# A Mamba mixer with a top-2 expert layer: the row statistics of the first layer norm move from VectorE to ScalarE

## What is computed

```python
def _layernorm(x, axis=-1, eps=1e-05):
    m = jnp.mean(x, axis=axis, keepdims=True)
    v = jnp.var(x, axis=axis, keepdims=True)
    return (x - m) / jnp.sqrt(v + eps)

# the mixer, on _layernorm(x)
xz = einsum('bld,ed->ble', h, in_proj_w); x, z = split(xz, 2)     # 2 x 1024 channels
xc = silu(sum_k conv1d_w[:, k] * xp[:, k:k + l, :])               # causal, 4 taps
dt_r, Bc, Cc = split(einsum('bld,ed->ble', xc, x_proj_w))         # 128, 16, 16
delta = softplus(dt_r @ dt_proj_w.T + dt_proj_bias); A = -exp(A_log)
h_t = h_{t-1} * exp(delta_t * A) + (delta_t * x_t) * B_t; y_t = <h_t, C_t>   # scan over the 512 tokens
out = ((y + xc * D_param) * silu(z)) @ out_proj_w.T

x = x + mixer(_layernorm(x))
x = x + experts(_layernorm(x))    # 8 experts, the top 2 of each token, silu(x w1) * (x w3), w2
```

## Time and profile before

| | |
|---|---|
| median of the runs shown | 4304.62 us |
| profiled execution | 4304.38 us, span 4302.6 us |
| busy, whole span | PE 91%, DVE 84%, POOL 60%, ACT 47% |
| mixer | up to about 2420 us |
| experts | from about 2420 us to the end |

### The profile page before, as it was taken

The page is one execution under the profiler, slowest core; times in us unless marked ns, Lnnn a source line. Parts: engine busy times, 40 slices in busy tenths (PEclk is TensorE's granted clock), DMA queues, the critical chain, the costliest instruction groups (busy, mean ns, idle before and its releaser), DMA issues. The chain is left out here.

```text
span 4302.6 us, 72404 instructions
## 1 busy us (share of the span) xinstructions
PE 3894.7 (91%) x25436; PEld 3380.4 (79%) x25436; DVE 3594.8 (84%) x5245; ACT 2043.5 (47%) x4314; POOL 2569.3 (60%) x2169
## 2 busy tenths in 40 slices
PE   6687889889988988898888599999999999999898
PEld 5565677677767776777676499999999999999886
DVE  5999998999999999999999588878878888788500
ACT  7677777777877778777766111111111111111100
POOL 3677778777876787687777244544545545445300
PEclk9888899999999999999998699999999999999999
DMA  4112353554445354535443555555555665655495
GB/s 162 64 40 93 119 174 114 172 165 151 142 157 174 116 167 162 174 111 177 162 150 101 176 187 176 192 182 181 185 176 181 195 184 177 190 176 190 136 331 192
DMA packets 422581, 694.11 MB, mean 161 GB/s; under 512 B 19680, under 2 KB 209760, under 8 KB 414048
## 3 DMA queue, kind: packets, MB, share of 16 engines
q1 hardware_dynamic: 406160, 655.24, 45.8%
q0 software_dynamic: 14768, 34.41, 4.2%
q10 hardware_dynamic: 1440, 1.81, 0.1%
HBM read 668.25 MB, written 45.95 MB: 166 GB/s over the span
## 5 line engine op out<-in xcount | busy, mean ns | idle before, releaser
L635 POOL TENSOR_TENSOR hs<-hs,bc 128x1024 f32<-128x1024 f32 x512 | 1214.5, 2372 | 307.6 <-DVE hs L1347 285.5
L1347 DVE TENSOR_TENSOR_SCAN hs<-dA,pU 128x1024 f32<-128x1024 f32 x512 | 1168.5, 2282 | 44.5 <-ACT dA L754 22.2
L754 ACT ACTIVATE dA<-delta,aneg 128x255 f32<-128x255 f32 x2048 | 852.1, 517 | 36.9 <-DVE hs L1347 33.7
L1146 PE MATMUL pY<-ident,hs 128*128 128x128 f32 x4096 | 566.1, 286 | 237.3 <-POOL hs L635 237.2
L1146 PEld LDWEIGHTS pY<-ident,hs 128*128 128x128 f32 x4096 | 488.4, 147 | 344.7 <-POOL hs L635 167.4
L1330 DVE TENSOR_TENSOR pU<-pZ,bc 128x1024 f32<-128x1024 f32 x512 | 629.7, 1230 | 30.5 <-issue 0.5
L1821 POOL TENSOR_TENSOR hsum<-hT 128x128 f32<-128x128 f32 x168 | 152.9, 910 | 585.1 <-DVE hT L2169 585.1
L1030 PE MATMUL pM<-xnT,win 128*128 128x256 f32 x1680 | 409.7, 400 | 30.9 <-DMA win<-in_w_in 25.1
L1030 PEld LDWEIGHTS pM<-xnT,win 128*128 128x128 f32 x1680 | 331.7, 203 | 80.8 <-issue 28.3
L2033 PE MATMUL ps<-xT,w1s 128*128 128x128 f32 x2688 | 357.8, 276 | 7.3 <-POOL xt L1837 5.3
L2033 PE MATMUL ps<-xt,su 128*128 128x128 f32 x2688 | 357.2, 276 | 0.0
(11 more groups left out here) (347 smaller groups left out, 7374.5 us busy)
## 6 DMA issues: line engine op xcount, KB each, us to landing
ew<-in_w SPq DMA_DIRECT2D x273, 512.0 KB, 4.1
w1s<-in_w SPq DMA_DIRECT2D x96, 1024.0 KB
w3s<-in_w SPq DMA_DIRECT2D x96, 1024.0 KB
w2s<-in_w SPq DMA_DIRECT2D x96, 1024.0 KB
win<-in_w_in SPq DMA_DIRECT2D x128, 512.0 KB, 4.7
bc<-bc_d SPq DMA_DIRECT2D x64, 1024.0 KB, 9.1
w1s<-in_w SPq DMA_DIRECT2D x32, 512.0 KB
w3s<-in_w SPq DMA_DIRECT2D x32, 512.0 KB
```

Source lines behind the costliest of these rows:

```text
L635: pool.tensor_tensor(hs[b][:, :, :], hs[b][:, :, :], bc[:, N + g * PN:N + (g + 1) * PN, :], ALU.mult)\
L754: e = act.activation(dA[k % NB][:, i, 1:T], delta[:, c, 1:T], ACT.Exp, scale=aneg[:, c, n:n + 1])
L1146: m = pe.matmul(pY[c % 2][:, t * P:(t + 1) * P], hs[k % NB][:, i, t * P:(t + 1) * P], ident[:, :], start=g == 0 and i == 0 and t == 0, sto ...
L1347: dve.tensor_tensor_scan(hs[b][:, :, :].rearrange("p n t -> p (n t)"), dA[b][:, :, :].rearrange("p n t -> p (n t)"), pU[:, :, :].rearrange ...
```

## The change

For the statistics that the steps make (those of the tokens of steps 2 to 15; the lead-in makes those of steps 0 and 1 as before) VectorE's `bn_stats` and `bn_aggr` go. In slot 14, behind `copy_z(2)`, ScalarE does for both tiles an Identity with scale -1/512 and an accumulated sum (minus the mean), waits for its own results, a Square with that as bias and an accumulated sum, waits again, and takes the root with 1/512 as scale. The elementwise results go to a buffer that is free by then (`waste`, `xnT`). The root of slot 13 and its table load go. VectorE waits for `sd1` at (15, 1) and not at (15, 0), the Newton step moves back by one place, its last part behind the last slot; the mean's sign turns in `scales`. The second layer norm is unchanged.

```diff
-        LN1S, BACKS, SPS, LNS = 8, 36, 4, 5
+        LN1S_FIRST, LN1S, BACKS, SPS, LNS = 8, 6, 36, 4, 5
...
+            def mean_of(rows, t, mv, to, step):
+                return act.activation(to, rows[:, t, 0:D], ACT.Identity, scale=-1.0 / D, accum_out=mv[:, t, 0:1]).then_inc(step, 1)
+            def squares_of(rows, t, mv, to, step):
+                return act.activation(to, rows[:, t, 0:D], ACT.Square, bias=mv[:, t, 0:1], accum_out=mv[:, t, 1:2]).then_inc(step, 1)
+            def root(mv, sdev, ready):
+                act.activation(sdev[:, :], mv[:, :, 1], ACT.Sqrt, bias=series[:, 2:3], scale=1.0 / D).then_inc(ready, 1)
...
-                    if u == 13 and ln1:
-                        ge(act, var1, s + 3)
-                        act.activation(tiny1[1][:, :], mv1[:, :, 1], ACT.Sqrt, bias=series[:, 2:3]).then_inc(sd1, 1)
                     if 12 <= u <= 15 and front:
                         copy_z(u - 12, f, szf)
+                    if u == SLOTS - 2 and ln1:
+                        ge(act, logits_mm, r + 1)
+                        ge(act, xf_in, 16 * s + 48)
+                        for t in range(TT):
+                            mean_of(xf, t, mv1, waste[t], moment1)
+                        ge(act, moment1, 2 * TT * s + TT)
+                        for t in range(TT):
+                            squares_of(xf, t, mv1, waste[t], moment1)
+                        ge(act, moment1, 2 * TT * s + 2 * TT)
+                        root(mv1, tiny1[1], sd1)
...
+            def variance(ch, mv, tiny):
+                ch.done(dve.tensor_scalar(tiny[0][:, :], mv[:, :, 1], 1.0 / D, EPS, ALU.mult, ALU.add))
...
+            def ln1_next(n, i):
+                if i == 0:
+                    ln1_chain[0] = Chain(ln1_step, 2 * LN1S_FIRST + LN1S * (n - 2))
+                    dve.wait_ge(sd1, n + 1)
+                ch = ln1_chain[0]
+                if i < 4:
+                    newton(ch, tiny1, i)
+                if i == 0:
+                    variance(ch, mv1, tiny1)
+                if i == 4:
+                    scales(ch, mv1, tiny1, 0, scale1, 1.0)
...
-                        if at in ((12, 2), (12, 3), (13, 1), (13, 2)):
-                            ln1(s + 2, ((12, 2), (12, 3), (13, 1), (13, 2)).index(at))
-                        if u == 15:
-                            ln1(s + 2, 4 + g)
+                        if u == 15 and g >= 1:
+                            ln1_next(s + 2, g - 1)
...
                 if ln1_too:
-                    ln1(s + 2, 8)
+                    ln1_next(s + 2, 3)
                 if picks:
-                    for i in range(4):
+                    pick(0)
+                if ln1_too:
+                    ln1_next(s + 2, 4)
+                if picks:
+                    for i in range(1, 4):
                         pick(i)
```

More of the change, by code:

```diff
@@ L233, in mixer @@
         sd1 = sem("sd1")
+        moment1 = sem("moment1")
         xn1 = sem("xn1")
@@ L696, in step @@
                 xcf, szs, szf = xc[1 - odd], sz[odd], sz[1 - odd]
+                waste = [xnT[odd][:, 2 * t:2 * t + 2, :].rearrange("p d q -> p (d q)") for t in range(TT)]
                 def read_dt(i):
@@ L1260, in aggregate, with scales @@
                 ch.done(i)
-            def scales(ch, mv, tiny, n, ready):
+            def scales(ch, mv, tiny, n, ready, sign=-1.0):
                 ch.settle()
                 ch.done(dve.tensor_copy(rs[n][:, :], tiny[4][:, :]))
-                dve.scalar_tensor_tensor(nb[n][:, :], tiny[4][:, :], -1.0, mv[:, :, 0], ALU.mult, ALU.mult)\
+                dve.scalar_tensor_tensor(nb[n][:, :], tiny[4][:, :], sign, mv[:, :, 0], ALU.mult, ALU.mult)\
                    .then_inc(ready, 1)
+            def variance(ch, mv, tiny):
+                ch.done(dve.tensor_scalar(tiny[0][:, :], mv[:, :, 1], 1.0 / D, EPS, ALU.mult, ALU.add))
             ln1_chain = [None]
             LN1_PARTS = 9
+            def ln1_next(n, i):
[9 more added lines that the diff above has]
+                    scales(ch, mv1, tiny1, 0, scale1, 1.0)
+                    assert ch.n == LN1S
             def ln1(n, i):
                 if i == 0:
-                    ln1_chain[0] = Chain(ln1_step, LN1S * n)
+                    ln1_chain[0] = Chain(ln1_step, LN1S_FIRST * n)
                 ch = ln1_chain[0]
@@ L1289, in ln1 @@
                 if i == 8:
-                    scales(ch, mv1, tiny1, 0, scale1)
-                    assert ch.n == LN1S
+                    scales(ch, mv1, tiny1, 0, scale1, -1.0)
+                    assert ch.n == LN1S_FIRST
             def step(s, odd):
```

## The result

The changed kernel took 4334.52 us (median of 4 runs, 4333.73 to 4335.66), the kernel before 4305.80 in the same comparison. The ratio is 1.0068, with a 95% interval of 1.0053 to 1.0082, so the change costs 0.7%. The profiled execution has a span of 4333.3 us, 30.7 more than before.

What follows compares the result with a forecast made beforehand. VectorE's sequence was taken to bound the mixer, with TensorE's backlog fixing when ScalarE is free in tile steps. Terms +35.2, -2.0 and -3.8 gave +29.4 us on a span of 4302.6: 4334 us predicted, range 4310 to 4350.

Steps and rivals of the forecast that it cites:

- T: Moment when ScalarE is free after the third copy of z; claimed fixed by TensorE's backlog in steps 3 to 13.
- the rooms: Time from ScalarE being free to VectorE's multiply of piece 31: 16.5 us over 11 steps, 1.5 us a step.
- row of waits: Second Square's wait for the last scan, 36.9 us in 11 steps; less about 1.85 us each gives 16.5 us.
- C: Time from ScalarE being free to the multiply of piece 31 with the added block: 4.7 us, between 4.1 and 5.4.
- The wait: VectorE at (15, 1) waits for ScalarE's root in steps 3 to 13; 11 x 4.7 - 16.5 = +35.2 us.
- The 3.8 us at the first scans: Waits of the next step's first scan for decays, in five steps, go when VectorE comes later: -3.8 us.
- Steps 0 to 2: Steps without an expert's tile: step 0 gains about 1.1 us, step 1 1.5, step 2 loses 0.6; together -2.0 us.
- The table switch that costs twice: Rival: ScalarE runs empty another 1.28 us at the table load behind an accumulation; 4348 us, chance 0.04.
- The read-outs of 0.6 us: Rival: each accumulated sum on ScalarE costs a small operation and a refill, 0.6 us; 4353 us, chance 0.07.
- The loss taken back inside the step: Rival: a later VectorE waits less for decays and logits, up to 24.6 us go; 4309 us, chance 0.09.
- The rival "faster": ScalarE's freed 2.9 us of slot 13 brings the root in time; VectorE gains up to TensorE's ranks: 4289 us, chance 0.08.

Runs made afterwards that it cites:

- queue edit: One weight load moved ahead in SyncE's queue: on the change 4296.22 us, on the kernel before 4292.61, on the change with ScalarE's block ahead of the `ysum` copy 4271.23.
- both kernels without the wait: The changed kernel with ScalarE's block moved ahead of the `ysum` copy, 4301.78 us; the changed kernel with VectorE's wait and Newton step behind the last slot, 4300.84.

## Why the prediction was right

4334 us were forecast and 4334.52 measured, and most steps hold one by one. That the two agree to half a microsecond is luck: beside the experiments the kernel before ran in 4297 to 4313 us, by the spans the change costs 30.7 us and not 29.4, by the medians 28.7, and a T that came 3.2 us late, which the forecast had not, was made up for in part by other misses (below).

*The bound and T.* In steps 3 to 13 T moved against the step's start by less than 0.3 us in seven, and by 3.2 us in sum over all eleven. VectorE's earlier arrival and ScalarE's freed time don't move it (root of slot 13 off: ratio 1.0001), TensorE's pause does (queue edit on the change: 38 us). The sum of the rooms by the row of waits was 16.5 us; the same eleven measured one by one give 16.4.

*The block.* C was forecast as 4.7 us between 4.1 and 5.4 and is 4.66: 2.90 for the four operations with their read-outs (forecast 3.0 with the two waits), 1.59 for load and root (1.58), 0.17 up to the multiply (0.15). The unknown term was the read-out of an accumulated sum: it has a row of its own, 0.19 to 0.20 us, overlapped by half with the next operation where one follows. The bound from the shortest ScalarE row was the right neighbour. The load starts 0.01 us after the last read-out ends, so there is no drain. The copy of `ysum` ahead of the block waits 2.4 us longer than before on average over these steps, and not 3: a part of ScalarE's freed time goes into the wait for TensorE at the second copy of z (0.96 us in step 6, 10.5 us in eleven steps).

*The wait.* Forecast: 4 to 6 us for the root in each of the eleven steps; measured: 4.0. Forecast for these steps: 35.2 - 3.8 = +31.4; measured: +33.3. The 3.8 us at the first scans came back as said (no such wait is left after the change). The rest is T, late by 3.2 us in sum: 1.6 in step 3 and 2.3 in step 13, where the third z product took 5.4 us and before 3.7, and 1.2 the other way in step 8, where it was the slow one before; it changes from run to run which steps these are. Against that stands 1.0 us in the stretch from the multiply to the next first scan, which is shorter by up to 0.3 us in ten of the eleven steps; why is open. Together: 11 x 4.66 less the room of 16.4 is 34.8, with 3.2 - 3.8 - 1.0 that makes 33.2, the 33.3 but for rounding.

*Steps 0 to 2.* Forecast -2.0, measured -2.6, with the parts wrong. Steps 0 and 1 gained 0.5 and 0.7 and not 1.1 and 1.5 (step 0 also started 0.2 sooner). VectorE came to the multiply of piece 31 only 0.7 us sooner in both; in step 1 a new wait of 0.44 us for decays is a part of that, the rest is open. And in these steps, without `pick` behind them, the later Newton part stands bare (0.2 us more between the last scan and `softplus`). Step 2 gained 1.3 where I had a loss of 0.6, because T came 3.1 us sooner against its step and not 1.28: both table loads and the root count there, since nothing on TensorE holds ScalarE. The rows:

```profile
465.28 0.58 ACT L781 ACTIVATE sz<-pM 128x512 f32<-128x512 f32 x1
465.76 0.63 ACT L688 ACTIVATE xnT<-xf 128x512 f32<-128x512 f32 x1
```

```profile
470.41 1.22 DVE L1370 TENSOR_TENSOR pU<-pZ,bc 128x1024 f32<-128x1024 f32 x1
```

against 470.19 and 473.04.

*The rivals.* The table switch that costs twice falls with the load of 1.28 us alone. The read-outs of 0.6 us fall with their rows. The loss taken back inside the step falls with the doubled Squares: 16 to 21 us for 18.6 us of work. The rival "faster" was priced wrongly, and this is the step of the prediction that failed without harm to the sum: a root in time would have given about 4301 and not 4289, as both kernels without the wait show. I had taken the room above the ranks as gain and had left out that the next step's start is TensorE's too. The advance of 3.2 us from which no step would lose was an average as well: the room between T and the multiply was 0.49 us in steps 8 and 11 and 2.88 in step 3.

## What to carry to other kernels

When work moves to an engine that is idle, look at what its idle time waits for, and put the work ahead of that wait and not behind it: the same block cost 0.7% behind a copy that waits for TensorE and nothing measurable ahead of it. The room that a new wait has is the distance between two rows of the trace, one on each engine, and a row of some later wait often holds it for all steps at once. Before counting a saving on the busiest engine, ask which other engine stands just behind it; here the saving was worth 2.5 us alone, not told from nothing, and 21 us once a 2 us pause of TensorE was gone.

## What the runs showed of the hardware

- A ScalarE operation with an accumulated sum is followed by a row of its own, ACTIVATION_READ_ACCUMULATOR, of 0.19 to 0.20 us; two operations over 128x512 with their read-outs took 1.34 us from the first start to the last end (1066.67 to 1068.01).
- TensorE's granted clock was 1.00 ahead of a 2 us pause and 0.67 over the product behind it in some steps, and 1.00 over it in others with a like pause (1.94 us in step 6); the product took 5.4 us against 3.7. With the pause gone it took 3.62 in all 15 steps of each kernel with the queue edit.
- VectorE's operation with two SBUF inputs made hardly any headway while GpSimd's multiply ran beside it: 1.21 us alone, 2.15 to 2.5 us with 1.1 to 1.4 us of overlap. The Trainium skill ("SBUF — State Buffer", "Who interferes with whom") says that such an operation contends with GpSimd's reads; the traces agree, and in them the price is about the whole overlap.
